# Two attention stages of a hybrid model: the layer norm ahead of the projections moves into the projections' program

## The chip, the cores and the metric

The kernel runs on one core of a Trainium2 chip. The metric is device time in microseconds (us) for one execution of the whole program. The core's engines are TensorE (PE in the profile; PEld is its weight load), VectorE (DVE), ScalarE (ACT), GpSimd (POOL) and SyncE (SP, which here issues most of the transfers). Each engine works through its own queue in program order; engines wait for one another through semaphores.

## What is computed

The reference is a chain of eight stages on a tensor `x` of 4 x 1024 tokens with 128 features: attention, a feed-forward network, a time and channel mix, the feed-forward network again, a second attention, mixtures of experts and a single-head attention. Each stage adds its result to `x`, and each gets a layer norm of `x`:

```python
def _layernorm(x, axis=-1, eps=1e-05):
    m = jnp.mean(x, axis=axis, keepdims=True)
    v = jnp.var(x, axis=axis, keepdims=True)
    return (x - m) / jnp.sqrt(v + eps)
...
x = x + _L0_attn_a_ref(_layernorm(x, axis=-1), ...) 
x = x + _L0_ffn_ref(_layernorm(x, axis=-1), ...)
x = x + _L0_attn_b_ref(_layernorm(x, axis=-1), ...)
x = x + _L0_ffn_ref(_layernorm(x, axis=-1), ...)
x = x + _L1_attn_a_ref(_layernorm(x, axis=-1), ...)
...
```

The change touches the first and the fifth stage, `_L0_attn_a_ref` and `_L1_attn_a_ref`. Both project the normalised `x` to a latent and to queries, and the latent to keys and values, and then attend causally.

## The kernel before

`x` lies in SBUF as `xs`, 32 tiles of 128 tokens. Everything ahead of the attention proper goes by chunks of 512 tokens (four tiles), of which there are eight (`NC`). The program is a sequence of blocks; a block gives each engine a queue, and the next block starts when all the queues have ended.

**The layer norm** (`layernorm`, tags `l0ln` and `l4ln` in these two stages) is a block of its own. For a chunk, DVE takes four `bn_stats` (L211), four `bn_aggr` (L215) and one addition (L217); ACT takes the square root (L249); DVE then the reciprocal (L226) and the product for the shift (L228), and normalises two of the four tiles into `ring` (L236), ACT the other two (L271); PE transposes the four tiles into PSUM (L296), and ACT copies the result to `hT` (L258), which holds the whole normalised and transposed `x`. DVE takes the statistics of a chunk while the chunk before it is under way.

**The projection** (`project`, tags `p0` and `p1`) is the next block in the first stage. In the fifth stage a small block `compose` stands between them; it loads weights, multiplies two pairs of them (L1251, L1254) and stores one product. In `p0` SP first issues twelve transfers (ten of weights and of their swapped halves, two of the tables of the rotation); PE, ACT and DVE wait for all of them (`s_ld`). Then, for each chunk:

- PE makes the latent in the PSUM bank `latp` (L1094), then the items that come from `hT` (L1105), waits for the latent's copy, makes the items that come from the latent, and last the values in `vp` (L1202 or L1271).
- ACT copies the latent to `lat` (L1125), and for each item the first bf16 piece "hi" (L1134) and the second "mid" (L1137).
- DVE takes for each item "rest" = value - hi (L1167), and "lo" = rest - mid (L1171); for rotated items first two products with cosine and sine and their sum (L1157, L1162); and last it copies the values (L1174).
- SP stores the three pieces of each item to DRAM (L1079), where the attention block reads them.

`p0` has four items: q (128 rows, from `hT`), qr (32 rows, rotated, from `hT`), k (128 rows, from the latent) and kr (32 rows, rotated, from the latent), so DVE has 14 operations a chunk. `p1` has four q items (128 rows each, from `hT`) and k, which is the latent itself, so DVE has 11 operations and ACT 11. The order on an engine is that of the lists `act_steps` and `dve_steps`: the "hi" of an item, then the "mid" of the item before it; the "rest" of an item, then the "lo" of the item before it. The loops over chunks are `Fori` loops of four turns with two chunks each.

Ahead of the first stage stands the block `fill`, in which SP issues 16 transfers of zeros (L123). Behind each projection stands the attention block.

Of the kernel before, what the change touches and what calls it, by code (L numbers as in the profile page):

```python
# [14 lines left out]
ALU = mybir.AluOpType  # L15
# [482 lines left out]


# [518 lines left out]
def project(nc, k, tag, hT, load, latent_w, latent_rows, items, make_values, vfree, split_latent=None, trig=None):  # L1018
# [3 lines left out]
    with ExitStack() as st:  # L1022
# [4 lines left out]
        if trig is not None:  # L1027
            cs = c.sb("cos_sin", [32, 2, T])
        lat = c.sb("lat", [P, 2, CH])
# [10 lines left out]
        s_passed = c.sem("product_passed")  # L1040
# [16 lines left out]
        order += [n for n in range(NI) if items[n].from_latent and items[n].w is not None]  # L1057
        pe_at = {n: 1 for n in range(NI)}
# [8 lines left out]
        def _(sp):  # L1067
# [5 lines left out]
            with sp.Fori(0, NC // 2) as i:  # L1073
# [11 lines left out]
        def _(pe):  # L1085
            pe.wait_ge(s_ld, 16 * nld)
            comp["pe"](pe)
            with pe.Fori(0, NC // 2) as i:
                for g in range(2):
# [3 lines left out]
                    pe.wait_ge(s_act, ACN * ch + act_at["lat", 0])  # L1093
                    pe.matmul(latp[0:latent_rows, :], latent_w(), h, start=True, stop=True).then_inc(s_pe, 1)  # L1094
                    for n in order:
                        it = items[n]
                        if it.from_latent:
# [3 lines left out]
                        pe.sem_inc(s_passed, 1)  # L1101
# [4 lines left out]
                    pe.wait_ge(s_act, ACN * (ch + 1) + act_at["lat", 0])  # L1106
                    pe.wait_ge(s_dve, DVN * (ch + 1))
                    pe.sem_inc(s_passed, 1)
# [5 lines left out]
        def _(act):  # L1114
# [3 lines left out]
            with act.Fori(0, NC // 2) as i:  # L1118
                for g in range(2):
                    ch = 2 * i + g  # L1120
                    for what, n in act_steps:
                        it = items[n]
                        if what == "lat":
                            act.wait_ge(s_pe, PEN * ch + 1)
                            act.activation(lat[0:latent_rows, g, :], latp[0:latent_rows, :], ACT.Copy).then_inc(s_act, 1)  # L1125

                            act.wait_ge(s_st[g], 16 * NI * (i + 1))
                        elif what == "hi":
# [5 lines left out]
                            act.activation(pcs[n][:, g, HI, :], source(n, it, g), ACT.Copy).then_inc(s_act, 1)  # L1134
                        else:
# [4 lines left out]
        def _(dve):  # L1140
            dve.sem_inc(s_dve, DVN)
            dve.sem_inc(s_st[0], 16 * NI)
            dve.sem_inc(s_st[1], 16 * NI)
            if trig is not None:
                dve.wait_ge(s_ld, 16 * nld)
            with dve.Fori(0, NC // 2) as i:
                for g in range(2):
                    ch = 2 * i + g
                    base = DVN * (ch + 1)

# [29 lines left out]
def layer0_attention(nc, k, ins, scr, xs, hT):  # L1180
    with ExitStack() as outer:
        co = Ctx(nc, outer, "a0")
        v = co.sb("v", [P, NT, P])
        with ExitStack() as wst:
# [16 lines left out]
            project(nc, k, "p0", hT, load, lambda: w[:, 0, :], P, items,  # L1201
# [11 lines left out]
def layer1_attention(nc, k, ins, scr, xs, hT):  # L1213
# [3 lines left out]
    with ExitStack() as outer:  # L1217
        co = Ctx(nc, outer, "a1")
        lt = co.sb("lt", [P, NT, LD])
        with ExitStack() as wst:  # L1220
# [49 lines left out]
            project(nc, k, "p1", hT, load, lambda: wd[:], LD, items,  # L1270
# [1421 lines left out]
def program(nc, ins, out):  # L2692
# [3 lines left out]
    with ExitStack() as st:  # L2696
# [23 lines left out]
        hst, hT = normalised("l0")  # L2720
        with hst:
            layer0_attention(nc, k, ins, scr, xs, hT)
# [12 lines left out]
        with hst:  # L2735
            layer1_attention(nc, k, ins, scr, xs, hT)
# [50 lines left out]
```

## Time and profile before

| what | us |
|---|---|
| median of 3 runs | 3193.41 (3193.13 to 3195.82) |
| the profiled execution, its own time | 3191.57 |
| its span, first to last instruction | 3188.6 |
| share of the span: PE, PEld, DVE, ACT, POOL | 74%, 39%, 55%, 39%, 13% |
| mean granted clock of TensorE | 0.864 |

The profile is one execution. Busy times are sums over all stages, and the stages differ; the two layer norms and the two projections have to be read from their own stretches. The clock row of a stretch is what the throttle granted, 1.00 for 2.4 GHz and 0.50 for 1.2 GHz. In the rows below a line number is that of the code printed above.

### The profile page before, as it was taken

How to read it: one execution, taken by the hardware profiler on the slowest of the kernel's cores; microseconds unless marked ns; L12 is line 12 of the kernel's file. 1: busy time of each engine (PE TensorE's matmuls, PEld its weight loads, DVE VectorE, ACT ScalarE, POOL GpSimd, SP SyncE). 2: the span in 40 equal slices, each digit the busy share in tenths (PEclk: the TensorE clock that was granted, in tenths of full speed). 3: DMA queues.
4: the chain of work that ended last, by engine and by line, in shares of the span. 5: the costliest groups of instructions: out<-in, count | busy, mean ns of one | idle time of the engine just before them, and what ended most of it. 6: DMA issues, size and time to landing. Idle time of an engine off the chain costs nothing. (4 is left out here: it accounts for less than half of the span.)

```text
span 3188.6 us, 48135 instructions
## 1 busy us (share of the span) xinstructions
PE 2362.7 (74%) x13512; PEld 1228.0 (39%) x13512; DVE 1765.6 (55%) x5580; ACT 1234.0 (39%) x1973; POOL 403.9 (13%) x452
## 2 busy tenths in 40 slices
PE   3649999999947328855999999999677382777382
PEld 1114344343325126532443434443254262554262
DVE  3756666666343896256565656666366324576223
ACT  2405455555524644443444444444323141343141
POOL 0000000000003000000000000000033553033554
PEclk9859999999968659877999999999888696888686
DMA  3272444443030000234111221121120142000144
GB/s 113 87 145 42 84 83 85 85 85 60 10 102 0 4 0 8 74 95 138 42 47 53 55 55 42 47 57 45 55 87 18 48 137 90 3 4 14 41 137 128
DMA packets 177882, 199.58 MB, mean 63 GB/s; under 512 B 36384, under 2 KB 117920, under 8 KB 177568
## 3 DMA queue, kind: packets, MB, share of 16 engines
q1 hardware_dynamic: 160000, 173.72, 21.9%
q0 software_dynamic: 9216, 19.02, 1.8%
q10 hardware_dynamic: 8448, 4.20, 0.4%
q8 instruction: 104, 1.70, 0.2%
q14 instruction: 114, 0.93, 0.1%
HBM read 127.09 MB, written 69.76 MB: 62 GB/s over the span
## 5 line engine op out<-in xcount | busy, mean ns | idle before, releaser
L810 ACT ACTIVATE at_probs<-at_score 128x1024 f32<-128x1024 f32 (+7 forms) x1024 | 654.6, 651 | 871.4 <-PE at_score L735 537.1
L835 DVE CUSTOM_DVE_ANT_0 at_masked<-at_mx,g_maskw 128x512 bf16<-128x512 f32 (+3 forms) x1024 | 483.2, 486 | 180.4 <-PE at_mx L701 176.2
L701 PE MATMUL at_mx<-at_K,at_Q 96*128 96x512 bf16 (+7 forms) x1536 | 466.5, 344 | 117.1 <-DVE at_mpart L835 39.4
L733 PE MATMUL at_score<-at_Q,at_K 96*128 96x512 bf16 (+7 forms) x1536 | 503.7, 332 | 27.0 <-issue 14.8
L735 PE MATMUL at_score<-at_Q,at_K 98*128 98x512 bf16 (+7 forms) x1536 | 506.7, 330 | 0.0
L831 DVE TENSOR_REDUCE at_mpart<-at_mx 128x1 f32<-128x512 f32 x512 | 353.8, 691 | 262.1 <-PE at_mx L701 242.8
L755 PE MATMUL at_outp<-at_probs,at_vop 128*32 128x512 f32 (+6 forms) x3072 | 445.5, 497 | 0.0
L701 PEld LDWEIGHTS at_mx<-at_K,at_Q 120*128 120x128 bf16 (+1 forms) x1536 | 148.2, 98 | 438.1 <-DVE at_mpart L835 197.4
L733 PEld LDWEIGHTS at_score<-at_Q,at_K 120*128 120x128 bf16 (+1 forms) x1536 | 149.7, 97 | 337.3 <-issue 181.1
L738 PE MATMUL at_score<-g_maskkq,g_identb 128*128 128x128 bf16 x1024 | 225.3, 220 | 0.0
L925 POOL MEMSET n_spread<- 16x128 f32 (+1 forms) x2 | 0.7, 355 | 1539.1 <-POOLq L536 1539.1
L755 PEld LDWEIGHTS at_outp<-at_probs,at_vop 128*32 128x32 f32 (+1 forms) x3072 | 125.1, 122 | 108.5 <-issue 61.3
L735 PEld LDWEIGHTS at_score<-at_Q,at_K 122*128 122x128 bf16 (+1 forms) x1536 | 151.1, 98 | 22.4 <-issue 2.7
L738 PEld LDWEIGHTS at_score<-g_maskkq,g_identb 128*128 128x128 bf16 x1024 | 101.7, 99 | 52.2 <-issue 3.4
L893 DVE COPY at_osb<-at_outp 128x1024 f32<-128x1024 f32 x48 | 58.8, 1225 | 77.6 <-PE at_outp L755 77.6
L835 DVE DVE_READ_ACCUMULATOR2_ANT at_mpart<- 128x1 f32 x1024 | 85.3, 83 | 0.3
L2464 POOL DMA_INDIRECT back<-m1e_ye,m1e_target x80 | 76.8, 961 | 55.4 <-DVE m1e_ye L2455 32.3
L2464 POOL DMA_INDIRECT back<-m0e_ye,m0e_target x80 | 76.8, 961 | 55.4 <-DVE m0e_ye L2455 32.2
L1495 PE MATMUL wkv_out<-wkv_wo,wkv_y 128*128 128x128 f32 x64 | 15.0, 429 | 90.8 <-DVE b_zt L1474 54.2
L683 POOL MEMSET at_K<- 2x8192 bf16 (+1 forms) x2 | 8.7, 4360 | 569.7 <-POOLq L1022 569.7
L1795 POOL DMA_INDIRECT buf<-m1x_z,m1x_slot x64 | 66.6, 1041 | 78.6 <-DVE m1x_slot L1934 60.3
L1795 POOL DMA_INDIRECT buf<-m0x_z,m0x_slot x64 | 66.5, 1038 | 77.9 <-DVE m0x_slot L1934 59.6
(488 smaller groups left out, 3413.7 us busy)
## 6 DMA issues: line engine op xcount, KB each, us to landing
at_Q<-q SPq DMA_DIRECT2D x192, 128.0 KB, 2.8
at_Q<-qr SPq DMA_DIRECT2D x72, 256.0 KB, 7.0
at_K<-kr SPq DMA_DIRECT2D x72, 256.0 KB, 8.6
q<-p_pieces SPq DMA_DIRECT2D x40, 384.0 KB, 3.2
at_K<-k SPq DMA_DIRECT2D x168, 64.0 KB, 2.3
buf<-g_zeros SPq DMA_DIRECT2D x32, 325.0 KB, 5.0
o<-at_osb SPq DMA_DIRECT2D x64, 128.0 KB
n_oc<-o SPq DMA_DIRECT2D x8, 1024.0 KB, 5.0
```

Source lines behind the costliest of these rows:

```text
L701: pe.matmul(bank[:, 0:hi - lo], Q0[0:R, g % 4, j, qt * P:(qt + 1) * P], K0[0:R, g % 4, j % KG, lo:hi], start=True, stop=True).then_inc(s_m ...
L733: pe.matmul(bank, K0[0:R0, g % 4, j % KG, kb * P:(kb + 1) * P], Q0[0:R0, g % 4, j, lo:hi], start=True, stop=False)
L735: last = pe.matmul(bank, K1[0:R1, g % 2, j % KG, kb * P:(kb + 1) * P], Q1[0:R1, g % 2, j, lo:hi], start=False, stop=not diag)
L738: last = pe.matmul(bank[:, 0:P], k.identb[:], k.maskkq[:], start=False, stop=True)
L755: last = pe.matmul(outp[M * j:M * (j + 1), half, lo - half * CH:CH], vop[:, g % 2, kb, j % VG, :], probs[:, kb % 2, j, lo:hi], start=(kb = ...
L810: act.activation(probs[:, kb % 2, j, kb * P:T], src, ACT.Exp, scale=cf.scale).then_inc(s_exp, 1)
L831: dve.reduce_max(mpart[:, part, j, qt:qt + 1], mx[:, u % 2, 0:w], AX).then_inc(s_mxf, 1)
L835: dve.tensor_tensor_reduce(masked[:, u % 2, 0:w], mx[:, u % 2, 0:w], k.maskw[:, CH - w:CH], 1.0, NEG, ALU.add, ALU.max, mpart[:, part, j, ...
L893: dve.tensor_copy(osb[:, g % 2, :], outp[:].rearrange("p h t -> p (h t)")).then_inc(s_oev, 1)
L1495: last = pe.matmul(out[:, t * P:(t + 1) * P], y[:, t * P:(t + 1) * P], wo[:], start=True, stop=True)
L1795: pool.indirect_dma_start(buf, bass.IndirectOffsetOnAxis(ap=slot[:, n, t:t + 1], axis=0), z[:, t, :], None).then_inc(s_out, 16)
L2464: pool.indirect_dma_start(back, bass.IndirectOffsetOnAxis(ap=target[:, e, t:t + 1], axis=0), ye[:, e % YR, t, :], None).then_inc(s_o[e % Y ...
```

## The change

The block `layernorm` is gone from the two attention stages (the other stages keep it). Its steps for one chunk become the methods of a class `Norm`, and `project` issues them in its own queues: the norm of chunk 0 and the statistics of chunk 1 ahead of the loop, and in the turn of chunk `ch` the rest of the norm of chunk `ch + 1` and the statistics of chunk `ch + 2`. `hT` becomes a tile of `project`. The transposes go to the PSUM bank `latp`, which the latent of the same chunk takes afterwards. The loops over chunks are written out in full instead of `Fori`. Two semaphore increments on PE (`s_passed`) fall away.

In the diff, cut to its core, `p1`'s transposes stand behind its last item and ahead of the values, as it has no item that PE makes from the latent; the lines for the ring tiles and the transposes themselves are those of the block before.

```diff
+class Norm:
...
+    def statistics(self, dve, ch):
+        for u in range(4):
+            dve.bn_stats(self.stats[:, ch % 2, u, :], self.src[:, 4 * ch + u, :]).then_inc(self.s_st, 1)
+        dve.wait_ge(self.s_st, 4 * ch + 4)
+        for u in range(4):
+            dve.bn_aggr(self.mv[:, ch, u, :], self.stats[:, ch % 2, u, :]).then_inc(self.s_ag, 1)
+        dve.wait_ge(self.s_ag, 4 * ch + 4)
+        dve.tensor_scalar(self.std[:, ch, :], self.mv[:, ch, :, 1], EPS, None, ALU.add).then_inc(self.s_var, 1)
+
+    def normalise(self, dve, ch):
+        dve.wait_ge(self.s_std, ch + 1)
+        dve.reciprocal(self.rstd[:, ch, :], self.std[:, ch, :]).then_inc(self.s_rstd, 1)
+        dve.wait_ge(self.s_rstd, ch + 1)
+        dve.scalar_tensor_tensor(self.shift[:, ch, :], self.mv[:, ch, :, 0], -1.0, self.rstd[:, ch, :], ALU.mult,
+                                 ALU.mult).then_inc(self.s_shift, 1)
+        if ch >= 2:
+            dve.wait_ge(self.s_tp, ch - 1)
...
+    def root(self, act, ch):
+        act.wait_ge(self.s_var, ch + 1)
+        act.activation(self.std[:, ch, :], self.std[:, ch, :], ACT.Sqrt).then_inc(self.s_std, 1)
+
+    def normalise_rest(self, act, ch):
+        act.wait_ge(self.s_shift, ch + 1)
...
+    def evacuate(self, act, ch):
+        act.wait_ge(self.s_tp, ch + 1)
...
+            act.activation(self.hT(ch // 2, ch % 2), self.turned(ch), ACT.Copy).then_inc(self.s_ev, 1)
+
+    def turn(self, pe, ch):
+        pe.wait_ge(self.s_rv, 2 * ch + 2)
+        pe.wait_ge(self.s_ra, 2 * ch + 2)
...
 def project(...):
+        norm = Norm(nc, c, k, xs, linear_view(hT), lambda ch: latp[:])
...
+        turn_at = next((n for n in order if items[n].from_latent), None)
...
             pe.wait_ge(s_ld, 16 * nld)
             comp["pe"](pe)
-            with pe.Fori(0, NC // 2) as i:
+            norm.turn(pe, 0)
+            for i in range(NC // 2):
...
-                    pe.wait_ge(s_act, ACN * ch + act_at["lat", 0])
+                    pe.wait_ge(norm.s_ev, ch + 1)
                     pe.matmul(latp[0:latent_rows, :], latent_w(), h, start=True, stop=True).then_inc(s_pe, 1)
                     for n in order:
...
+                        if n == turn_at:
                             pe.wait_ge(s_act, ACN * (ch + 1) + act_at["lat", 0])
+                            if ch + 1 < NC:
+                                norm.turn(pe, ch + 1)
...
...
             act.wait_ge(s_ld, 16 * nld)
             comp["act"](act)
             act.sem_inc(s_act, ACN)
+            norm.root(act, 0)
+            norm.normalise_rest(act, 0)
+            norm.evacuate(act, 0)
+            norm.root(act, 1)
...
                             act.activation(lat[0:latent_rows, g, :], latp[0:latent_rows, :], ACT.Copy).then_inc(s_act, 1)
+                            if ch + 1 < NC:
+                                norm.normalise_rest(act, ch + 1)
+                            if ch + 2 < NC:
+                                norm.root(act, ch + 2)
...
                             act.activation(pcs[n][:, g, HI, :], source(n, it, g), ACT.Copy).then_inc(s_act, 1)
+                            if n == 0 and ch + 1 < NC:
+                                norm.evacuate(act, ch + 1)
...
+            norm.statistics(dve, 0)
+            norm.normalise(dve, 0)
+            norm.statistics(dve, 1)
...
+                    if ch + 1 < NC:
+                        norm.normalise(dve, ch + 1)
+                    if ch + 2 < NC:
+                        norm.statistics(dve, ch + 2)
                     dve.wait_ge(s_st[g], 16 * NI * (i + 1))
                     for what, n in dve_steps:
...
-        hst, hT = normalised("l0")
-        with hst:
-            layer0_attention(nc, k, ins, scr, xs, hT)
+        layer0_attention(nc, k, ins, scr, xs)
...
-        hst, hT = normalised("l4")
-        with hst:
-            layer1_attention(nc, k, ins, scr, xs, hT)
+        layer1_attention(nc, k, ins, scr, xs)
```

## Rows read from the trace of the kernel before

**Rows 1.** Stretches by start:end, busy (count) by engine, clock, DMA share, GB/s.
```profile
27.95:50.28 22.33, 8.88 (x32) 5.72 (x32) 17.37 (x104) 13.93 (x33) 0.00 (x0) 1.00 0.11 39
50.28:58.30 8.02, 0.00 (x0) 0.00 (x1) 0.00 (x0) 0.00 (x0) 0.00 (x0) 1.00 0.29 74
58.30:152.38 94.08, 69.22 (x176) 22.25 (x176) 75.70 (x120) 39.29 (x72) 0.00 (x0) 0.91 0.24 80
1358.98:1380.98 22.00, 8.89 (x32) 5.73 (x32) 17.22 (x104) 13.94 (x33) 0.00 (x0) 0.53 0.00 0
1402.50:1462.49 59.99, 43.41 (x112) 15.57 (x112) 51.60 (x88) 47.63 (x88) 0.00 (x0) 0.93 0.72 213
```

**Rows 2.** Timeline of the first layer norm: start, duration, engine, line [idle before].
```profile
27.95 0.87 DVE L211 BATCH_NORM_STATS2 l0ln_stats<-g_xs 128x6 f32<-128x128 f32 x4 [27.95 <-PEq L104]
29.58 0.21 ACT L249 ACTIVATE l0ln_std<-l0ln_std 128x4 f32<-128x4 f32 x1 [0.34 <-DVE l0ln_std L217]
30.96 0.18 DVE L226 RECIPROCAL l0ln_rstd<-l0ln_std 128x4 f32<-128x4 f32 x1
31.26 0.60 DVE L236 TENSOR_SCALAR l0ln_ring<-g_xs,l0ln_mv,l0ln_rstd 128x128 f32<-128x128 f32 x2
31.38 0.88 ACT L271 ACTIVATE l0ln_ring<-g_xs,l0ln_shift,l0ln_rstd 128x128 f32<-128x128 f32 x2
31.77 0.87 DVE L211 BATCH_NORM_STATS2 l0ln_stats<-g_xs 128x6 f32<-128x128 f32 x4
32.38 1.11 PE L296 MATMUL l0ln_turned<-g_ident,l0ln_ring 128*128 128x128 f32 x4 [32.38 <-ACT l0ln_ring L271]
33.20 0.17 DVE L217 TENSOR_SCALAR l0ln_std<-l0ln_mv 128x4 f32<-128x4 f32 x1
34.47 0.57 ACT L258 ACTIVATE l_hT<-l0ln_turned 128x512 f32<-128x512 f32 x1
```

**Rows 3.** Timeline of the start of p0: first product, first rest.
```profile
50.28 0.35 SPq L1069 DMA_DIRECT2D a0w_w<-in_L_attn_a_W_kv_down  x1
58.30 2.07 PE L1094 MATMUL p_latp<-l_hT,a0w_w 128*128 x2 [8.91 <-ACTq L1117]
62.74 0.69 DVE L1167 TENSOR_TENSOR p_rest<-p_bank,p_pieces 128x512 f32<-128x512 f32 x1 [15.44 <-ACT p_pieces L1134]
```

**Rows 4.** p0: timeline of a middle chunk; DVE's and PE's waits from 74 to 152.
```profile
84.99 0.57 ACT L1134 ACTIVATE p_pieces<-p_bank 128x512 bf16<-128x512 f32 x1
86.08 0.67 DVE L1167 TENSOR_TENSOR p_rest<-p_bank,p_pieces 128x512 f32<-128x512 f32 x1
97.11 0.67 DVE L1167 TENSOR_TENSOR p_rest<-p_bank,p_pieces 128x512 f32<-128x512 f32 x1
...
DVE p_rest L1167 <- ACT p_pieces L1134: 9.7, 14, 0.7
...
PE p_bank L1105 <- ACT p_lat L1125: 18.8, 7, 3.6
```

**Rows 5.** Timeline of p1: its start, and the first rest of chunks 2 and 3.
```profile
1402.74 1.91 PE L1094 MATMUL p_latp<-l_hT,a1w_wd 128*32 x2 [3.93 <-ACTq L1117]
1407.32 0.69 DVE L1167 TENSOR_TENSOR p_rest<-p_bank,p_pieces 128x512 f32<-128x512 f32 x1 [7.75 <-ACT p_pieces L1134]
1408.23 0.60 ACT L1134 ACTIVATE p_pieces<-p_bank 128x512 bf16<-128x512 f32 x1 [0.94 <-PE p_bank L1105]
1409.84 0.43 PE L1271 MATMUL p_vp<-g_ident,p_lat 32*128 32x32 f32 x4
1421.66 1.29 DVE L1167 TENSOR_TENSOR p_rest<-p_bank,p_pieces 128x512 f32<-128x512 f32 x2
1428.47 1.29 DVE L1167 TENSOR_TENSOR p_rest<-p_bank,p_pieces 128x512 f32<-128x512 f32 x2
```

**Rows 6.** Timeline of the first feed-forward block, where ACT first waits for weights.
```profile
946.23 1.28 ACT L481 ACT_TABLE_LOAD   x1 [5.11 <-ACTq L474]
```

**Rows 7.** Stretches within p0, one chunk long; columns as in the first group.
```profile
118.00:129.00 11.00, 10.41 (x22) 3.14 (x22) 9.47 (x15) 4.84 (x10) 0.00 (x0) 0.71 0.26 89
129.00:140.00 11.00, 7.57 (x22) 2.58 (x22) 9.42 (x16) 4.84 (x10) 0.00 (x0) 1.00 0.26 89
```

More of the change, by code:

```diff
@@ L1015, in __init__, with project @@
         self.rows, self.w, self.from_latent, self.dst, self.w2 = rows, w, from_latent, dst, w2
-def project(nc, k, tag, hT, load, latent_w, latent_rows, items, make_values, vfree, split_latent=None, trig=None):
+def project(nc, k, tag, xs, load, latent_w, latent_rows, items, make_values, vfree, split_latent=None, trig=None):
     NI = len(items)
@@ L1028, in project @@
             cs = c.sb("cos_sin", [32, 2, T])
+        hT = c.sb("hT", [P, N])
         lat = c.sb("lat", [P, 2, CH])
@@ L1072, in _ @@
                 sp.dma_start(cs[:, 1, :], trig[1]).then_inc(s_ld, 16)
-            with sp.Fori(0, NC // 2) as i:
+            for i in range(NC // 2):
                 for g in range(2):
@@ L1087, in _ @@
             comp["pe"](pe)
-            with pe.Fori(0, NC // 2) as i:
+            norm.turn(pe, 0)
+            for i in range(NC // 2):
                 for g in range(2):
@@ L1105, in _ @@
                         pe.matmul(banks[n][0][0:it.rows, :], it.w(), rhs, start=True, stop=True).then_inc(s_pe, 1)
-                    pe.wait_ge(s_act, ACN * (ch + 1) + act_at["lat", 0])
+                    if turn_at is None:
+                        pe.wait_ge(s_act, ACN * (ch + 1) + act_at["lat", 0])
+                        if ch + 1 < NC:
+                            norm.turn(pe, ch + 1)
                     pe.wait_ge(s_dve, DVN * (ch + 1))
-                    pe.sem_inc(s_passed, 1)
                     for t in range(4):
@@ L1117, in _ @@
             act.sem_inc(s_act, ACN)
-            with act.Fori(0, NC // 2) as i:
+            norm.root(act, 0)
+            norm.normalise_rest(act, 0)
+            norm.evacuate(act, 0)
+            norm.root(act, 1)
+            for i in range(NC // 2):
                 for g in range(2):
@@ L1143, in _ @@
             dve.sem_inc(s_st[1], 16 * NI)
+            norm.statistics(dve, 0)
+            norm.normalise(dve, 0)
+            norm.statistics(dve, 1)
             if trig is not None:
                 dve.wait_ge(s_ld, 16 * nld)
-            with dve.Fori(0, NC // 2) as i:
+            for i in range(NC // 2):
                 for g in range(2):
@@ L1177, in _, with layer0_attention @@
                         ins.then_inc(s_dve, 1)
-def layer0_attention(nc, k, ins, scr, xs, hT):
+def layer0_attention(nc, k, ins, scr, xs):
     with ExitStack() as outer:
@@ L1200, in layer0_attention @@
                      Item(32, lambda: wr[:, 1, :], True, scr.kr0, lambda: wr[:, 3, :])]
-            project(nc, k, "p0", hT, load, lambda: w[:, 0, :], P, items,
+            project(nc, k, "p0", xs, load, lambda: w[:, 0, :], P, items,
                     lambda pe, lt, bank: pe.matmul(bank, lt, w[:, 3, :], start=True, stop=True), P,
@@ L1269, in layer1_attention @@
                      for r in range(4)] + [Item(LD, None, True, scr.k1)]
-            project(nc, k, "p1", hT, load, lambda: wd[:], LD, items,
+            project(nc, k, "p1", xs, load, lambda: wd[:], LD, items,
                     lambda pe, l, bank: pe.transpose(bank, l, k.ident[0:LD, 0:LD]), LD)
```

39 lines of the change are left out of this document (35 added, 4 removed).

## The prediction

> **What bounds the kernel now.** I read the stretches first [rows 1]. The norm of the first stage takes 22.33 us, from 27.95 to 50.28, that of the fifth 22.00 us, and nothing of the projection runs beside them. Behind the first lie 8.02 us in which no engine works: SP issues p0's weights, and the first product starts when they are in [rows 3]. Then p0 runs 94.08 us, with DVE busy for 75.70, PE for 69.22, ACT for 39.29. p1 runs 59.99 us, with DVE at 51.60 and ACT at 47.63. So the question is whether a projection has room on DVE for the 17.37 us that DVE works in a norm.
>
> Next I followed one chunk on DVE [rows 4]. From the first "rest" of a chunk, at 86.08, to that of the next, at 97.11, are 11.03 us: this is p0's period. Over some seven chunks DVE's only sizeable wait is for the "hi" pieces of ACT, 9.7 us in 14 waits of at most 0.7, which is 1.4 us a chunk. They stand in the middle of the chunk, behind each rotated sum. At the boundary of two chunks DVE doesn't wait at all. In p1 the period is 1428.47 - 1421.66 = 6.81 us [rows 5], with DVE and ACT both nearly full. DVE thus sets both periods, and what is put into its queue between two chunks lengthens them by at least its own time.
>
> **What is removed.** Both norm blocks with their barriers: 22.33 and 22.00 us [rows 1]. The block that multiplies weights ahead of p1 only moves forward.
>
> **What a turn of the loop gains on DVE.** The norm of chunk ch+1 and the statistics of chunk ch+2 stand in front of the first "rest" of chunk ch. In the norm block this same run goes from the reciprocal at 30.96 to the end of the variance step at 33.20 + 0.17 = 33.37 [rows 2], 2.41 us. That isn't all. ACT's queue holds, in this order, the latent's copy, two ring tiles, the root for chunk ch+2, and only then the first "hi" of chunk ch. The root waits for the variance step, which is the last thing in DVE's run; DVE's first "rest" waits for that "hi". So behind DVE's 2.41 us come the root, 0.21 [rows 2], and the "hi", 0.57 [rows 4], while DVE stands still: 2.41 + 0.21 + 0.57 = 3.19, with handovers of some hundredths that the overlap of the two ACT operations pays for. I take 3.2 us a turn. Its lower end is 2.41, if the wait were covered; nothing in the queues covers it, so I stay at the upper. Turns 1 to 5 pay in full. In turn 6 there is no chunk left for statistics: from the reciprocal to ACT's ring tiles 0.42, these 0.88 [rows 2], the "hi" 0.57, so 1.9. Turn 7 pays nothing. Turn 0 has its share in the head, below.
>
> **The head of p0.** SP's issues now follow the block of zeros at once, at 27.95 for 50.28, and the weights are in 8.02 later, at 35.97 (up to 2 us more if the zeros still fill the queue; I take none, since the last weights are issued 5 us behind). DVE has the first statistics long by then, but ACT waits for the weights ahead of the root. That a table load isn't pulled ahead of such a wait is seen in the feed-forward block: 1.28 us, behind 5.11 of waiting [rows 6]. So: load 1.28, root 0.21, reciprocal to the end of ACT's ring tiles 31.38 + 0.88 - 30.96 = 1.30, transposes 1.11, copy to hT 0.57 [rows 2], and five handovers of 0.05 to 0.12, in all 4.8 us. The first product starts at 40.8, and the first "rest" follows it by 62.74 - 58.30 = 4.44 [rows 3], at 45.2. It stood at 62.74, so it leads by 17.5. Meanwhile DVE does the norm of chunk 1 and the statistics of chunk 2, which takes it to about 43.4, ahead of the "hi", so turn 0 adds nothing.
>
> p0 then pays 5 x 3.2 + 1.9 = 17.9, less some 0.5 because its first chunk, slowed by a PE at half clock (a pair of passes takes 2.07 us [rows 3]), now has more time: 17.4. **Sum for p0: -17.5 + 17.4, nothing.** PE's four transposes, 1.1 us at most, lie in its spare time: it waits 2.7 us a chunk for the latent [rows 4]. The stores of SP, and their semaphores, keep their order and get longer apart.
>
> **The head of p1.** No weights are waited for here, and the table load runs beside the first statistics, as in the norm block, where the statistics start at 27.95 and the root at 29.58 [rows 2]. There the reciprocal came only at 30.96, as the statistics of chunk 1 went first; now it follows the root at 29.84, so all behind it comes 1.12 sooner: transposes end at 33.49 - 1.12 = 32.37, the copy at 33.04, which is 5.1 us after the block's start. The product starts 5.2 us after the block's start where it was 1402.74 - 1402.50 = 0.24. Lead: 22.0 - 5.0 = 17.0.
>
> **A new wait in p1's first chunk.** ACT's copy to hT of chunk 1 stands between the first "hi" and the second. It waits for the transposes, and these stand in PE's queue behind all four q products of chunk 0. In the profile what stands there, the first transposes for the values, starts at 1409.84, 7.1 us after the first product; with 0.6 to 1.1 for the transposes and 0.6 for the copy the second "hi" starts 8.4 to 8.9 us after it, where it was 1408.23 - 1402.74 = 5.5 [rows 5]. Queued behind: every other piece of chunk 0 on ACT, and DVE's "rest" that needs them. That is 2.9 to 3.4; if PE's clock rises earlier, because the transposes of chunk 0 come before, it may be 2.0. I take 2.7. In later chunks the q products are done before the turn begins, each needing only a "rest" of the chunk before, and the wait is gone.
>
> In turns 1 to 5 that copy (0.57) also takes a place on ACT just where p1 needs the second "hi" right behind the first; between 0 and 0.5, I take 0.2, as ACT then waits less for the "rest" that follows. In turn 6 the copy waits for its transposes, 0.7. So p1 pays 2.7 + 5 x 3.4 + 1.9 + 0.7 = 22.3. **Sum for p1: -17.0 + 22.3 = +5.3.**
>
> The loops written in full cost nothing that a row shows. For the removed increments on PE and the loops' branches I take 0.2 off.
>
> **Total.** -0.1 + 5.3 - 0.2 = +5.0 us on the profiled execution's own 3191.57 gives 3196.6; the median of the runs lies 1.84 above that execution, so the forecast is 3198.4.
>
> **Rival 1, faster: the norm falls into DVE's holes.** If DVE's 2.41 us used the 1.4 us a chunk in which it waits in p0, and the root didn't hold up the "hi", a turn would cost 1.0 in p0 and 2.4 in p1: p0 -17.5 + 5 x 1.0 + 1 = -11.5, p1 -17.0 + 2.7 + 5 x 2.4 + 1 = -1.3, and the time 3180.6. Against it: the holes are inside the chunk and the norm is a block between chunks, so only the order of the queue would have to be other than the diff says. The Trainium skill, Perfetto Trace Analysis, section Optimization Strategy, says that stages with different most-contended engines may gain from interleaving. By that rule the time would be this rival's; the trace speaks against it here, as DVE is the busiest engine of both stages [rows 1].
>
> **Rival 2, slower: PE at half clock.** PE's wait for the latent in p0, up to 3.6 us [rows 4], grows to some 5 in a period of 14.2. In the stretch where the granted clock was 0.71 PE was busy for 10.41 of 11.00 us, and DVE's work didn't suffer [rows 7]. With the transposes, and all at 1.2 GHz, a chunk needs 14 passes (two for each of seven products) of 2.07 / 2 = 1.0 or a little less, some 13, with 1.1 for the transposes and an estimated 1 to 2 for the values: 15 to 16 in a period of 14.2. Where this exceeds the period, PE becomes the bound: about 1 us in each of six chunks, in p1 less, 0.3 a chunk, and 1 to 2 more for the first chunk. That adds some 9 us: 3207. It decides only if the clock is low for most of the stage; a PE that is busy all the time speaks against that. The Trainium skill, TensorE: Matmul & The Clock Gate, section Why this matters for your kernels, warns that idle gaps between bursts bring the clock down. A clock of 0.71 in one chunk and 1.00 in the next [rows 7] agrees with that.
>
> **How the numbers follow.** Forecast case 0.75, rival 1 0.09, rival 2 0.16. A measurement of this kernel can tell about 0.2%, 6.4 us, so the bounds are 3187.0 and 3199.8. The forecast's own range, from the ends above, is 3193 to 3202: 0.57 of its chance lies within the bounds, 0.17 above, 0.01 below. Slower is then 0.17 + 0.16 = 0.33, the same 0.57, faster 0.09 + 0.01 = 0.10. The range, 3189 to 3207, leaves out rival 1 and half of rival 2.
>
> **What would show it.** In the profile after: the first "rest" of p0 near 45 and of p1 17 us sooner against its block; a period near 14.2 in p0 and 10.2 in p1; DVE waiting some 0.8 us for the first "hi" of each chunk, released by the root before it; one long wait of ACT for the transposes in p1's first chunk. Wrong would be: a period near 12 in p0 (rival 1), waits of DVE for PE's products (rival 2), or a head of p0 longer than 17 us.

## The result, and the profile after

| | before | after |
|---|---|---|
| median of 17 runs each | 3191.80 us | 3199.26 us |
| ratio | 1 | 1.0027, 95% interval 1.0019 to 1.0034 |
| profiled execution (span) | 3191.57 us (3188.6) | 3206.48 us (3203.2) |

By the ratio the change costs 8.6 us, 6.1 to 10.9 by the interval, a little more than 0.2%; the two medians lie 7.5 us apart. A second series of 11 runs gave 1.0024 (1.0015 to 1.0033), 7.7 us. The forecast was 5.0 us more than before, the time given 3198.4, the range 3189 to 3207. The profiled execution of after lies 7.2 us over its own median, so I use it for the order of the work and the length of a chunk, and several executions for where the time went.

Stretches of after, each with its length, the busy time by engine (PE, weight loads, DVE, ACT, POOL, with counts), the clock, and the DMA share: p0's head up to its first product, p0 from there, the weights' block of p1, and p1.

```profile
27.98:41.09 13.11, 1.09 (x5) 0.72 (x5) 3.61 (x22) 3.02 (x6) 0.00 (x0) 1.00 0.39 109
41.09:152.81 111.72, 74.89 (x204) 26.80 (x204) 89.17 (x202) 50.03 (x100) 0.00 (x0) 0.88 0.20 68
1366.68:1388.35 21.67, 8.89 (x64) 8.25 (x64) 1.39 (x3) 0.23 (x1) 0.00 (x0) 0.54 0.36 74
1388.35:1472.88 84.53, 57.23 (x144) 22.09 (x144) 68.61 (x192) 60.35 (x121) 0.00 (x0) 0.78 0.51 152
```

Against [rows 1]: 22.33 + 8.02 + 94.08 have become 13.11 + 111.72. What the norm gave up ahead of the stage, the stage took back almost to the microsecond. In p1, 22.00 + 59.99 have become 84.53, 2.5 more.

The timeline of p0's start (start, duration, engine, line, idle time before it and what ended it), to be laid beside [rows 2, 3]:

```profile
36.35 1.28 ACT L545 ACT_TABLE_LOAD   x1 [36.35 <-DMA p_cos_sin<-in_rope_sin]
...
40.44 0.60 ACT L563 ACTIVATE p_hT<-p_latp 128x512 f32<-128x512 f32 x1 [1.27 <-PE p_latp L570]
41.09 2.07 PE L1170 MATMUL p_latp<-p_hT,a0w_w 128*128 128x512 f32 x2 [0.69 <-ACT p_hT L563]
...
45.29 0.69 DVE L1263 TENSOR_TENSOR p_rest<-p_bank,p_pieces 128x512 f32<-128x512 f32 x1 [1.77 <-ACT p_pieces L1221]
```

The first "rest" of p0 stands at 45.29 instead of 62.74. The table load, and everything of the first chunk's norm that follows it on ACT, waited for the last of p0's transfers, a table of the rotation, to land.

A turn of p0's loop, on DVE and ACT:

```profile
85.58 0.15 DVE L533 RECIPROCAL p_rstd<-p_std 128x4 f32<-128x4 f32 x1
...
87.68 0.17 DVE L529 TENSOR_SCALAR p_std<-p_mv 128x4 f32<-128x4 f32 x1
87.88 0.20 ACT L545 ACTIVATE p_std<-p_std 128x4 f32<-128x4 f32 x1 [1.03 <-DVE p_std L529]
87.99 0.58 ACT L1221 ACTIVATE p_pieces<-p_bank 128x512 bf16<-128x512 f32 x1
88.67 0.69 DVE L1263 TENSOR_TENSOR p_rest<-p_bank,p_pieces 128x512 f32<-128x512 f32 x1 [0.83 <-ACT p_pieces L1221]
```

From the reciprocal to the "rest" are 3.09 us: 2.27 of DVE's work, then 0.83 in which DVE stands while ACT does the root and the "hi". Before, the "rest" followed the last values with no wait [rows 4]. From "rest" to "rest" (74.37 to 88.67) a chunk now takes 14.30 us, where it took 11.03. DVE's waits in p0 from 59 to 153, in total, how many, and the longest:

```profile
DVE p_rest L1263 <- ACT p_pieces L1221: 16.7, 20, 1.0
```

14 of the 20 are the holes behind the rotated sums, as in [rows 4], the rest is the first "hi" of the turns.

The same in p1: its first chunk, and the turns.

```profile
1388.35 0.87 DVE L524 BATCH_NORM_STATS2 p_stats<-g_xs 128x6 f32<-128x128 f32 x4 [3.06 <-PEq L1325]
...
1393.31 1.92 PE L1170 MATMUL p_latp<-p_hT,a1w_wd 128*32 128x512 f32 x2 [0.69 <-ACT p_hT L563]
...
1398.04 0.69 DVE L1263 TENSOR_TENSOR p_rest<-p_bank,p_pieces 128x512 f32<-128x512 f32 x1 [2.37 <-ACT p_pieces L1221]
...
1401.26 0.60 ACT L563 ACTIVATE p_hT<-p_latp 128x512 f32<-128x512 f32 x1 [3.33 <-PE p_latp L570]
1402.38 0.69 DVE L1263 TENSOR_TENSOR p_rest<-p_bank,p_pieces 128x512 f32<-128x512 f32 x1 [3.65 <-ACT p_pieces L1221]
...
1421.04 0.69 DVE L1263 TENSOR_TENSOR p_rest<-p_bank,p_pieces 128x512 f32<-128x512 f32 x1 [0.82 <-ACT p_pieces L1221]
...
1430.82 0.69 DVE L1263 TENSOR_TENSOR p_rest<-p_bank,p_pieces 128x512 f32<-128x512 f32 x1 [0.83 <-ACT p_pieces L1221]
```

ACT's long wait for the transposes of the second chunk is there, 3.33, and DVE's "rest" behind it waits 3.65. Later chunks take 9.78 us (before, 6.81 [rows 5] and 6.84 by turns).

So the two projections account for +2.9 us in this execution, and the runs say 7.7 to 8.6. The rest had to be looked for in lines that the change doesn't touch.

### The profile page after: what moved, and what is told of

Same layout as the page of the kernel before. It is cut to its first block and busy times, and to the rows that moved or that the text cites. A ratio compares the mean times of both kernels' runs of the same rounds, so it can differ in the third digit from the quotient of the medians.

```text
span 3203.2 us, 47112 instructions
## 1 busy us (share of the span) xinstructions
PE 2373.3 (74%) x13512; PEld 1233.1 (38%) x13512; DVE 1764.4 (55%) x5580; ACT 1231.4 (38%) x1973; POOL 401.6 (13%) x452
## 5 line engine op out<-in xcount | busy, mean ns | idle before, releaser
L808 PE MATMUL at_score<-at_Q,at_K 98*128 98x512 bf16 (+7 forms) x1536 | 507.9, 331 | 4.9 <-issue 4.9
L808 PEld LDWEIGHTS at_score<-at_Q,at_K 122*128 122x128 bf16 (+1 forms) x1536 | 151.5, 99 | 22.4 <-issue 2.5
L966 DVE COPY at_osb<-at_outp 128x1024 f32<-128x1024 f32 x48 | 58.8, 1225 | 76.6 <-PE at_outp L828 76.6
```

The costliest lines, as they stand in the source:

```text
L808: last = pe.matmul(bank, K1[0:R1, g % 2, j % KG, kb * P:(kb + 1) * P], Q1[0:R1, g % 2, j, lo:hi], start=False, stop=not diag)
L966: dve.tensor_copy(osb[:, g % 2, :], outp[:].rearrange("p h t -> p (h t)")).then_inc(s_oev, 1)
```

## The experiments

### Where the rest lies: both kernels again

> The kernel before, once more, for the scatter of the stretches that no line of the change touches. Theory A (the new stalls of TensorE in the attentions come from where its program lies): this run repeats the profile of before: stage at0 764.8 us within 1, stage at1 to the sixth norm 1218.0 within 1, one issue wait of 3.6 to 3.9 us at each turn of at1's loop over batches and no second one. Rival (scatter of the run): stage at0 or at1 differs from the first profile by 2 us or more, and the second issue wait of 2.3 to 2.6 us appears here too. Ratio to before 1.000.

> The changed kernel, once more. Theory A (the program's place): this run repeats the profile of after: at0 768.8 us within 1, at1 to the sixth norm 1222.4 within 1, the second issue wait (2.3 and 2.6 us) at both turns of at1's loop. Rival (scatter): those stretches come back to 764.8 and 1218.0, or move by 2 us or more. Ratio 1.0027.

Measured: 3191.77 us for the kernel before (ratio 0.9999, 0.9988 to 1.0011), 3199.13 for the changed one (1.0024). Each stretch goes from DVE's first instruction in a block to its first in the next, but the one behind wkv begins where DVE's last addition there ends, and that of p1 where the second feed-forward's last addition ends; one profiled execution to a column. Not listed are wkv itself, 101.9 us in all five, and the second feed-forward, 58.8 to 60.1; sem_only, further down, is the changed kernel but for the number of a semaphore.

| stretch, us | before | before_again | after | after_again | sem_only |
|---|---|---|---|---|---|
| norm and p0 | 135.77 | 135.67 | 136.11 | 137.15 | 137.05 |
| at0 | 720.15 | 722.74 | 723.30 | 721.90 | 722.25 |
| from n0 to wkv | 187.41 | 187.76 | 188.80 | 188.30 | 187.62 |
| end of wkv to second feed-forward | 125.43 | 126.37 | 127.94 | 127.94 | 128.07 |
| norm and p1, with the weights' block | 111.54 | 110.58 | 114.00 | 114.04 | 114.02 |
| at1 | 824.57 | 823.63 | 828.80 | 828.43 | 828.67 |
| n1 to the end | 895.06 | 894.34 | 895.15 | 890.02 | 888.60 |

The expectations of these two and the next two kernels count at0 to the norm behind it and at1 to the sixth norm; by that count before_again has 767.2 and 1216.7, after_again 766.3 and 1219.3, so neither repeats within 1 us, and to that extent the rival is right. In the table at0 scatters by 2.6 us within one kernel, and the last stretch by 6.6: the 4.0 us that at0 seemed to have lost in the first pair of profiles were scatter. Three rows are steady. By their means, p1 has +3.0, the stretch behind wkv +2.1, and at1 +4.5. p0 has +1.0, of the size of its own scatter (136.11 to 137.15 in the changed kernel). Together these are 10.6, more than the runs' 7.7 to 8.6; in these executions the last stretch was 3.4 us shorter after the change, which is within its scatter.

The stretch behind wkv first. The channel mix there starts with products of 128x512. Two stretches of 10 us around its start, TensorE alone (busy time and count, granted clock, DMA share), before and then after:

```profile
1199.80:1209.80 10.00, 6.39 (x12) 0.66 0.12 30
```

```profile
1205.20:1215.20 10.00, 6.42 (x8) 0.52 0.11 28
```

In the same busy time TensorE gets through 12 products before and 8 after: the clock comes up from 1.2 to 2.4 GHz later, and the channel mix is 1.4 us longer (70.07 against 68.64). TensorE's work ahead of it, the transposes of the norm, is the same in both, but it comes at another time. In that norm, at the third chunk, DVE has an idle time after the change that it didn't have before, in a line that no edit touched and with no wait that the profile shows (before, then after):

```profile
1181.90 0.60 DVE L236 TENSOR_SCALAR b_ring<-b_zt,b_mv,b_rstd 128x128 f32 x2
```

```profile
1187.12 0.60 DVE L236 TENSOR_SCALAR b_ring<-b_zt,b_mv,b_rstd 128x128 f32 x2 [0.34 <-issue]
```

after_again, sem_only and all the changed kernel's variants below have it too (0.34 us; best and best_shift 0.14, at a later instruction); the kernel before and its variants, four executions, have none. In the changed kernel the transposes behind it come up to 0.45 us later, and the channel mix starts 36.9 us after wkv's last instruction on DVE, for 36.5. That this is what brings the clock up later is likely and not shown: in best the start comes after 36.6 us, and TensorE gets through 12 products as in the kernel before; after_shift has 36.8 and 10.

In at1 the profile shows the loss in TensorE's timeline, where its loop over the batches turns: before, and then after, at the first turn.

```profile
1699.15 0.61 PE L733 MATMUL at_score<-at_Q,at_K 96*128 96x512 bf16 x1 [3.62 <-issue]
1699.55 0.63 PE L735 MATMUL at_score<-at_Q,at_K 98*128 98x512 bf16 x1
```

```profile
1708.83 0.39 PE L806 MATMUL at_score<-at_Q,at_K 96*128 96x512 bf16 x1 [3.87 <-issue]
1711.51 0.58 PE L808 MATMUL at_score<-at_Q,at_K 98*128 98x512 bf16 x1 [2.29 <-issue]
```

"issue" is time in which the engine waited for nothing that the profile shows. Every turn has one such wait, in both kernels. It is the loop's branch: of the six branches that TensorE takes or passes at the end of a turn in after's two attentions, the median lasts 3.69 us, and of DVE's six 0.06 (shortest, median and longest in ns, then the first and last start); TensorE's 0.08 are of a last turn, which goes on behind the loop.

```profile
L680 PEldq COMPARE_BRANCH  x6: 83/3693/3917, 393.0 to 2112.9; - x6
L680 DVEq COMPARE_BRANCH  x6: 55/63/72, 393.6 to 2113.4; - x6
```

After has a second wait, an instruction later, 2.29 us at the first turn and 2.62 at the second, in lines that no edit touched. after_again repeats it with 2.81 and 2.34, before_again has none. Theory A: TensorE's program lies elsewhere since the projections are written out and two norm blocks are gone, and in this place the instructions behind the loop's branch come late.

### The place of TensorE's program

Increments of a semaphore that nobody waits for move what stands behind them in TensorE's program. In the project function, both kernels:

```
+            for _pad in range(PAD[tag][0]):
+                pe.sem_inc(s_pad, 1)
             pe.wait_ge(s_ld, 16 * nld)
...
                     last.then_inc(s_pe, 1)
+            for _pad in range(PAD[tag][1]):
+                pe.sem_inc(s_pad, 1)
```

> The kernel before with nothing changed but 56 semaphore increments that nobody waits for at the start of p0's TensorE program (it waits there for the weights) and 48 at the end of p1's, so that the branches of both attentions' loops over batches stand at the same instruction of TensorE's program as in the changed kernel (1471 and 4265 instead of 1415 and 4161). Theory A (the program's place): at0 768.8 instead of 764.8 and at1 1222.4 instead of 1218.0, the second issue wait of 2.3 to 2.6 us appears, ratio 1.0015 to 1.003. Rival 1 (addresses in SBUF, since hT no longer lies under the attentions): as before, 764.8 and 1218.0, ratio 1.000. Rival 2 (scatter): either, without order. Cost of the increments themselves: hidden in p0, at most 3 us in p1.

> The changed kernel with 72 semaphore increments that nobody waits for at the start of p0's TensorE program and 80 at the start of p1's, while TensorE waits there for weights or for DVE: the branch of at0's loop comes to instruction 1543 (1415 of before and 128), that of at1's to 4417 (4161 and 256). Theory A (the program's place, if what counts repeats with a power of two): at0 764.8 and at1 1218.0 as before, no second issue wait, about 8 us less than the changed kernel: ratio 1.000 to 1.0008. If the place counts in another way, at0 and at1 come to some third value. Rival (SBUF addresses): 768.8 and 1222.4 as in the changed kernel, ratio 1.0027.

before_pad: 3190.95 us, ratio 0.9997 (0.9986 to 1.0007); at1 824.38, no second wait. Theory A's expectation failed as I had put it: the same count of instructions ahead of the loop doesn't bring the wait. This run alone would also fit its rival 1, the addresses in SBUF; the next ones rule that out, as the wait goes in them while the addresses stay the changed kernel's. after_pad: 3204.13, 1.0037 (1.0024 to 1.0051); there at1 fell to 824.54 and the second wait went. But its total rose, since the increments weren't hidden in p1 (the product behind them, then the increments: how many, shortest, median and longest in ns, first and last start):

```profile
1402.15 1.09 PE L570 MATMUL p_latp<-g_ident,p_ring 128*128 128x128 f32 x4 [16.10 <-issue]
...
L1166 PEldq EVENT_SEMAPHORE  x80: 51/51/51, 1389.7 to 1401.8; - x80
```

The 80 of them run from 1389.7 to 1401.8, 0.15 us apart; the rest of the 16.10 us is, but for 0.3, the end of the block before (the next expectation divides the whole by 80 and so has 0.20). p1 became 8.0 us longer. So the same increments went where TensorE has nothing to do for 36.6 us, the start of wkv:

```
 # wkv, tensor engine (after_shift: 152, shift_24: 24, shift_64: 64)
+            for _ in range(152):
+                pe.sem_inc(s_pad, 1)
             pe.wait_ge(s_ld, 48)
```

(From here on the expectations name at1's end wrongly: their 822 to 828.6 us are those of at1's row in the table, up to n1.)

> The changed kernel with 152 semaphore increments that nobody waits for at the start of wkv's TensorE program, where TensorE waits 36.6 us for its first vectors (152 at the 0.20 us that 80 of them took apiece in after_pad is 30 us). The second attention's program for TensorE then stands where it stood in after_pad; nothing else moves. Theory A (part of the loss is where TensorE's program lies in the second attention): no issue wait of 2.3 to 2.8 us beside the 3.4 to 3.9 at each of the two turns of at1's loop, at1 to the sixth norm's block 824.5 us instead of 828.6, the rest as in the changed kernel; about 4 us less than it, ratio 1.0010 to 1.0015. Rival (in after_pad the later start of p1 did it, not the place): 828.6, ratio 1.0024 to 1.0027.

Measured: 3192.13 us, ratio 1.0004 (0.9994 to 1.0014), at1 822.02 us. The turn of the loop:

```profile
1706.06 0.39 PE L806 MATMUL at_score<-at_Q,at_K 96*128 96x512 bf16 x1 [3.69 <-issue]
1706.28 0.38 PE L808 MATMUL at_score<-at_Q,at_K 98*128 98x512 bf16 x1
```

The change without the second wait can't be told from the kernel before. That is 6 to 7 us less than the changed kernel and not the 4 expected: at1 comes out 2 us below the kernel before too, as TensorE is busy there for 771.3 us with the same 4416 products, against 773.1 to 774.2. So not all of it is the second wait. Two shorter shifts, and a control for the one thing that the shifted kernels have beside the increments, a further semaphore, which moves the numbers of all that follow:

> The changed kernel with 24 increments in wkv's TensorE program instead of after_shift's 152. If what counts is the place within a block of 64 (or 32, or 128) instructions, 24 acts as 152 did (152 is twice 64 and 24): no second issue wait in at1, 822 to 824.5 us. If it is the distance in itself, a shift as small as this leaves both second waits, 828.6.

> The changed kernel with 64 increments in wkv's TensorE program. If what counts is the place within a block of 64 instructions, the second issue waits of 2.3 to 2.8 us stay at both turns of at1's loop, 828.6 us. If within a larger block, or the distance in itself, they go or change.

> The changed kernel with the semaphore of the shifted kernels set aside in wkv and no increment of it: the numbers of the semaphores in the second attention move by one as they do there, and TensorE's program keeps its place. Theory A (the place of TensorE's program): both second issue waits of 2.3 to 2.8 us stay, at1 to the sixth norm's block 828.6 us. Rival (the numbers of the semaphores did it in the shifted kernels): the second waits go, 822 us.

One execution each: at1 822.17 with 24 increments and 822.09 with 64, with no second wait at either turn. So the place within a block of 64 instructions isn't what counts. With the semaphore alone, 828.67 and the second wait:

```profile
1706.91 0.39 PE L806 MATMUL at_score<-at_Q,at_K 96*128 96x512 bf16 x1 [3.43 <-issue]
1710.11 0.58 PE L808 MATMUL at_score<-at_Q,at_K 98*128 98x512 bf16 x1 [2.81 <-issue]
```

That settles what: of the kernels made from the changed one, those with TensorE's program in the changed kernel's place (after, after_again, sem_only, and root_late below; best below is one instruction off) have the second wait, and the four that shift it by 24 to 152, with best_shift below, haven't. What the place does can be read from the weight loads (PEld) at the turn. In after the load for L808 still comes at once, at 1708.83, and its product late. In best, whose program for TensorE runs one instruction more ahead of at1, that load itself is late (its line is L816 there):

```profile
1708.83 0.10 PEld L808 LDWEIGHTS at_score<-at_Q,at_K 98*128 98x128 bf16 x1
```

```profile
1683.75 0.10 PEld L816 LDWEIGHTS at_score<-at_Q,at_K 98*128 98x128 bf16 x1 [3.15 <-issue]
```

With one instruction more ahead, the stop comes one instruction earlier in the turn: it stands at a fixed place of TensorE's program, a few instructions behind the branch's target. after_again, sem_only and root_late have it where after has it. The Trainium skill, Runtime: NRT & Kernel Launch, section Instruction fetch mechanics, says that an engine's program is fetched ahead in blocks of 256 instructions and only in sequence, and that a taken branch to a place that isn't held has to wait for its block. The branches of 3.3 to 4.3 us at each turn of the attentions' loops, in every kernel here, agree, and so does a stop at a fixed place just behind the target, if a block ends there. That blocks are of 256 instructions no run here shows, and before_pad, with an equal count but the projections' loops not written out, speaks at least against counting instructions in the built program.

### Written-out loops alone

In the kernel before, each of the four loops of the project function:

```
-            with dve.Fori(0, NC // 2) as i:
+            for i in range(NC // 2):
```

> The kernel before with the four loops of the projections' programs written out, as in the changed kernel, and nothing else; norms where they were. If writing out is what made the hole behind a rotated sum 0.82 us instead of 0.70: two holes in each of 8 chunks, p0 1.9 us longer than 94.1 and its chunk 11.27 instead of 11.03. If the norm's steps made it: 94.1 and 11.03. By the theory that at1's second issue wait comes with the place of TensorE's program, this third place gives either of the two levels (824 or 828 us), with the waits to match. Ratio to before 1.000 to 1.002.

Measured: 3194.08 us, ratio 1.0009 (0.9999 to 1.0020); norm and p0 137.84 us, +2.1, nearly as by the first theory (+1.9), of which a chunk of 11.20 instead of 11.03 to 11.04 (11.27 was expected) gives 1.2 and the first chunk, 13.03 instead of 12.15, the rest. DVE's waits in p0 from 74 to 152, for which [rows 4] showed 9.7 in 14 with at most 0.7:

```profile
DVE p_rest L1167 <- ACT p_pieces L1134: 11.5, 14, 0.8
```

So the hole behind a rotated sum, 0.69 to 0.70 in the loop, is 0.82 in the same program written out: 0.16 us a chunk, with no norm step in it. The trace shows what is added: written out, the "hi" behind a rotated sum has a semaphore instruction of its own ahead of it in ACT's queue (14 in the seven chunks), and the "rest" one in DVE's; in the loop there is none at either place.

```profile
L1131 ACTq EVENT_SEMAPHORE  x14: 17/17/17, 78.1 to 150.5; - x14
```

In the chunk from 97.8, from the end of DVE's sum to the start of the "hi" it takes 0.09 us instead of the loop's 0.03, and from the end of the "hi" to the "rest" 0.10 instead of 0.03. p1 lost nothing by writing out (110.15). at1 (825.82) hasn't the second wait in its place; it has shorter ones, 0.73 and 1.13 us, five products further on, which the profile puts down to DVE. The runs' own ratio isn't clear of 1; the reading rests on the stretch.

### The root behind the first copy

```
 # scalar engine, in the chunk's steps
                                 norm.normalise_rest(act, ch + 1)
-                            if ch + 2 < NC:
-                                norm.root(act, ch + 2)
...
                                 norm.evacuate(act, ch + 1)
+                            if n == 0 and ch + 2 < NC:
+                                norm.root(act, ch + 2)
```

> The changed kernel with ScalarE's root of the chunk after next moved from the front of the chunk's first copy to behind it and behind the copy of the transposed chunk. Theory (the root is what DVE's 0.83 us wait for the first hi is made of, six turns in p0 and five in p1): that wait goes in p0, period 14.30 to about 13.5, p0 some 5 us less; in p1 9.78 to about 9.2 (the second hi follows late by the copy and the root), some 3 us less; ratio to the changed kernel 0.9975, to before 1.000. Rival (the first hi is late because of the two rows on ScalarE and DVE's statistics, not the root): the wait stays over 0.5 us and the period falls by less than 0.3 us.

Measured: 3191.47 us, ratio 1.0003 (0.9992 to 1.0013), which is 0.0021 to 0.0024 below the changed kernel's, as expected. A turn of p0:

```profile
72.54 0.57 ACT L1219 ACTIVATE p_pieces<-p_bank 128x512 bf16<-128x512 f32 x1
73.46 0.17 DVE L529 TENSOR_SCALAR p_std<-p_mv 128x4 f32<-128x4 f32 x1
73.54 0.69 DVE L1263 TENSOR_TENSOR p_rest<-p_bank,p_pieces 128x512 f32<-128x512 f32 x1
73.93 0.20 ACT L545 ACTIVATE p_std<-p_std 128x4 f32<-128x4 f32 x1
```

The "hi" is done under DVE's statistics, the "rest" follows them with no wait, and the root comes last. p0's chunk fell from 14.30 to 13.38, p1's from 9.78 to 9.07, with 0.42 of the second "hi"'s lateness left. The root's place in ACT's queue was the 0.83. p0's stretch is 132.36 us, 3.8 to 4.8 less than the changed kernel's for some 5 expected, p1's 110.95, 3.1 less.

### The norm's steps where the engines wait

```
 # PE and ACT: the first chunk's norm ahead of the wait for the weights
+            norm.turn(pe, 0)
             pe.wait_ge(s_ld, 16 * nld)
 # DVE, p0: behind the two rotated sums of a chunk
+                        if what == "rot" and ch + 2 < NC:
+                            (norm.sums if n == rotated[0] else norm.variance)(dve, ch + 2)
 # ACT: all four vectors of a chunk (p0) or two (p1) behind hi 0 or hi 1,
 # the transposed chunk's copy behind hi 1 or hi 2, the root ahead of the last mid
+                            if n == rest_at and ch + 1 < NC:
+                                norm.normalise_rest(act, ch + 1)
+                            if n == copy_at and ch + 1 < NC:
+                                norm.evacuate(act, ch + 1)
...
+                            if n == NI - 1 and ch + 2 < NC:
+                                norm.root(act, ch + 2)
```

> The changed kernel with the norm's steps put where the engines wait: p0's sums of a chunk behind its first rotated sum and the variances behind its second (holes of 0.82 us), all four normalised vectors of p0 on ScalarE, the first chunk's norm ahead of the wait for the weights, the root before the chunk's last mid, and the transposed chunk's copy behind hi 1 (p0) or hi 2 (p1). Theory (p0 and p1 are DVE's row of operations and its waits for ScalarE): p0's period from 14.30 to 11.5 to 12, its first product at about 37 instead of 41; p1's from 9.78 to about 8.8, without the 3.65 us wait in its first chunk; about 28 us less than the changed kernel, ratio to before 0.992 to 0.995. Rival (ScalarE's row becomes the bound, with all four vectors on it): p0's period stays above 13, ratio above 0.997.

> The kernel best with after_shift's 152 increments at the start of wkv's TensorE program. Theory A (the place of TensorE's program in the second attention): the second issue waits of 2.9 and 2.4 us at the turns of at1's loop go, at1 to the sixth norm's block falls from 828.5 to 822 to 824.5 us, the rest stays; median 3172 to 3176, ratio to before 0.994 to 0.995. Rival (the second wait belongs to the state in which p1 leaves the engines): 828.5, ratio 0.996.

best: 3178.94 us, ratio 0.9961 (0.9948 to 0.9974), faster than both kernels, but 20 us below the changed one and not 28, and outside the 0.992 to 0.995 expected, into which only its interval reaches. p0's stretch is 121.92 us instead of 136 to 137, p1's 107.22 instead of 114. DVE's timeline at a turn of p0 and at two of p1:

```profile
77.17 0.67 DVE L1280 TENSOR_SCALAR a_v<-p_vp 128x512 f32<-128x512 f32 x1
77.77 0.15 DVE L540 RECIPROCAL p_rstd<-p_std 128x4 f32<-128x4 f32 x1
...
78.04 0.69 DVE L1273 TENSOR_TENSOR p_rest<-p_bank,p_pieces 128x512 f32<-128x512 f32 x1
...
80.55 0.85 DVE L529 BATCH_NORM_STATS2 p_stats<-g_xs 128x6 f32<-128x128 f32 x4
81.45 0.68 DVE L1273 TENSOR_TENSOR p_rest<-p_rot,p_pieces 32x512 f32<-32x512 f32 x1
...
1396.09 1.29 DVE L1273 TENSOR_TENSOR p_rest<-p_bank,p_pieces 128x512 f32<-128x512 f32 x2
...
1405.12 1.29 DVE L1273 TENSOR_TENSOR p_rest<-p_bank,p_pieces 128x512 f32<-128x512 f32 x2
```

And its waits in p0, from 52 to 138:

```profile
DVE p_rest L1273 <- ACT p_pieces L1227: 6.0, 12, 0.8
DVE p_rot L1263 <- PE p_bank L1192: 2.7, 4, 1.1
```

A turn of p0 now costs DVE 0.27 us (77.77 to 78.04), and at this turn the sums fill the hole behind the rotated sum whole; over p0 6.0 us of such holes remain. Yet the chunks of p0 took 11.8 to 13.4 us, not 11.5 to 12: four vectors in ACT's queue delay the transposes, and DVE now waits for TensorE's products as well (2.7 us in 4 waits), which it didn't before. In p1 the two first "rest" run back to back again, and a chunk takes 9.04 (8.8 expected), hardly less than root_late's 9.07: there most of the gain over root_late is in the first chunk, 10.20 for 12.52. The moves of best were not run one by one. best had at1's second waits, 2.86 and 2.37. With the 152 increments of after_shift they are gone, at1 takes 824.01 instead of 828.52, and best_shift has 3170.92 us, ratio 0.9939 (0.9925 to 0.9953): a little below what was expected, 19 us under the kernel before.

## Why the prediction was right, and where it was wrong

**The bound.** That DVE sets both periods, and that the norm put between two chunks adds its own length there, held: no run contradicts it, and rival 1 (the norm falls into the holes by itself) is out. It takes the order of best to put it there.

**p0.** The first "rest" was forecast at 45.2 and came at 45.29: a lead of 17.45 for 17.5. A turn was 3.09 for 3.2 (the chunk's 14.30 less 11.21, the length of the written-out chunk that has no turn). Turn 6 was 13.06 - 11.21 = 1.85 for 1.9, and the first chunk gave back 0.6 for 0.5 in the first profile. The step that failed: "The loops written in full cost nothing that a row shows". They cost 0.16 us a chunk, 1.3 in eight, as unrolled_only shows (2.1 there with its longer first chunk), a semaphore instruction more at each handover of a rotated item. With it p0 stands at +1.0 by the table instead of -0.1.

**p1.** Its head: from the end of the feed-forward block the first "rest" comes 17.1 us sooner, for 17.0. The first chunk's wait for the transposes: its 13.22 us, less the old 7.48 and a turn of 2.97, leave 2.8 for 2.7. The mis-sized terms are the turns, 9.78 - 6.81 = 2.97 for 3.4, and turn 6, 8.53 - 6.81 = 1.72 for 1.9 + 0.7. A turn there is 2.27 of DVE's work (not 2.41 as in the norm block [rows 2]) and a wait of 0.83, 3.10 as in p0; the 0.2 us by which the second "hi" was to be late don't come on top, the rest of the chunk being 0.13 shorter than before. Turn 7, forecast at nothing, cost 7.34 - 6.81 = 0.53. So the stage lost 3.0 and not 5.3.

**The mechanism of the turn** was named in the right place: DVE 2.3, then the root, then the "hi". root_late moves the root alone and takes the 0.83 us off.

**Rival 2** (PE at half clock) didn't come in the changed kernel: in p0 from 59 to 153 DVE waits for ACT's pieces and not for products (the list of waits above). Its condition came in part: in p1 the granted clock of the stretches 1411 to 1421, 1421 to 1431 and 1431 to 1441 was 0.74, 0.94 and 0.72, where before each chunk from 1408 to 1448.5 had 1.00, and still DVE waited for no product. Products did make DVE wait in best, 2.7 us in 4 waits.

**What was missing altogether.** The projections cost some 4.0 us by the table, for 5.0 forecast, but the whole costs 7.7 to 8.6. The missing term is in unchanged code: 4.5 us in at1, where TensorE's program came to lie so that it waits twice where the loop turns. after_shift, which moves it and nothing else of the work, brings the ratio from 1.0024 to 1.0027 down to 1.0004, some 2 us of it beside the wait. Another 2 us are in the stretch behind wkv, of which 1.4 go with a clock that comes up later. That the time forecast, 3198.4, was so close to the 3199.3 measured was luck: one term was too large, another absent, and the forecast stood on a median of three runs, 3193.41, where 17 give 3191.80. What I had given most chance, no difference that can be told, holds for the change with the place corrected, not for the kernel as it stood.

The Trainium skill, Perfetto Trace Analysis, section Optimization Strategy, says to look for the gaps on the engine that matters and for what blocks it there. In this case the changed kernel left DVE's gaps of 0.82 us open; best, which among other moves puts the statistics into them, agrees with that advice, with 121.92 us for p0 instead of 136 to 137. 5.0 us of that are the earlier first "rest", 40.27 for 45.29.

## What to carry to other kernels

Work that is moved off a serial stretch into a loop costs its full length there if it stands as one run between two iterations on the engine that sets the period; put its pieces behind that engine's own waits, and put whatever another engine owes it, here a root of 0.2 us, behind what the next iteration needs first. When a change writes out loops or removes blocks, compare the unchanged stretches too: a steady difference there, repeated in a second execution, can be larger than the change itself, and moving the program by a few instructions in an idle place tells whether the code's place is at fault. And a difference of 4 us between two profiled executions says little in a stretch where one kernel's own scatter is 2.6.

## What the runs showed of the hardware that was not expected

- TensorE's branch at each turn of an attention's loop over batches lasts 3.3 to 4.3 us in all kernels (DVE's 0.06), and in one place of its program it waits 2.1 to 2.9 us more, behind the branch, at a place that stays the same when the program is one instruction longer. A shift by 24 instructions removes it.
- Semaphore increments alone on TensorE take 0.15 us each (80 from 1389.7 to 1401.8).
- DVE's wait for ACT's copy of a 32x512 tile, each waiting only for the other, is 0.69 to 0.70 us in a loop and 0.82 in the same program written out, in p0, where each of the two has a semaphore instruction of its own ahead of it; in p1 writing out cost nothing.
- At the start of the channel mix TensorE's clock comes up later in the changed kernel, 8 products instead of 12 in the same 6.4 us of busy time, with the same work ahead of it, 0.4 us later.
